# Four graph layers on one core: in two gather passes GpSimd waits behind each eight gathers until they have landed

## The reference

```python
def _gat(x, src, dst, W, a_src, a_dst, b, concat, n):
    H, C = a_src.shape
    h = (x @ W).reshape(n, H, C)
    s_src = (h * a_src).sum(-1)
    s_dst = (h * a_dst).sum(-1)
    e = jax.nn.leaky_relu(s_src[src] + s_dst[dst], NEG_SLOPE)
    m = jax.ops.segment_max(e, dst, num_segments=n)
    ex = jnp.exp(e - m[dst])
    denom = jax.ops.segment_sum(ex, dst, num_segments=n)
    alpha = ex / (denom[dst] + 1e-16)
    out = jax.ops.segment_sum(h[src] * alpha[:, :, None], dst, num_segments=n)
    ...
```

## Time and profile before

| what | us |
|---|---|
| time, median of 3 runs (lowest to highest) | 10376.22 (10362.24 to 10378.53) |
| span of the profiled execution | 10471.3 |
| first pass, first to last gather's start | 1414.9 to 2587.5 |
| second | 2831.3 to 4017.3 |
| third | 4278.4 to 5450.8 |
| fourth | 5701.3 to 7527.9 |

### The profile page before, as it was taken

One profiled execution on the slowest core, in us unless ns is written; L12 is line 12 of the kernel. 1 busy time (PEld: TensorE's weight loads), 2 busy tenths in 40 slices (PEclk: granted clock), 3 DMA queues, 4 the chain that ended last, 5 costly groups with the idle time before them and its releaser, 6 DMA issues. The chain is left out here.

```text
span 10471.3 us, 116347 instructions
## 1 busy us (share of the span) xinstructions
PE 6049.5 (58%) x41783; PEld 5358.8 (51%) x41783; DVE 3913.4 (37%) x8586; ACT 2215.5 (21%) x5791; POOL 5606.2 (54%) x5805
## 2 busy tenths in 40 slices
PE   3555634455456565455554666666669999943232
PEld 2445524444355554344442666665649999932222
DVE  5455523333334443344443333333332222232223
ACT  0000012222133332122220333333311111111111
POOL 6666366666666665666666566666540000036665
PEclk7555557766578876576665778888759999975555
DMA  4554252221133331233322444444319888821111
GB/s 160 168 169 166 81 43 54 55 53 48 41 94 98 99 97 38 78 102 94 103 77 66 120 119 124 121 122 121 92 35 359 339 334 334 334 97 24 23 23 23
DMA packets 437827, 1237.73 MB, mean 118 GB/s; under 512 B 161169, under 2 KB 226706, under 8 KB 394048
## 3 DMA queue, kind: packets, MB, share of 16 engines
q1 hardware_dynamic: 200226, 740.56, 20.1%
q0 software_dynamic: 237024, 489.72, 17.8%
HBM read 1099.82 MB, written 127.51 MB: 117 GB/s over the span
## 5 line engine op out<-in xcount | busy, mean ns | idle before, releaser
L1252 PE MATMUL ps<-pool 128*106 128x128 f32 (+2 forms) x19344 | 3021.3, 319 | 1685.2 <-issue 1171.0
L1252 PEld LDWEIGHTS ps<-pool 128*106 128x106 f32 (+2 forms) x19344 | 2773.5, 196 | 1889.3 <-issue 1406.2
L1210 ACT ACTIVATE ACC<-ps 72x256 f32 (+1 forms) x2418 | 1012.2, 419 | 2573.8 <-remote 1653.5
L469 POOL DMA_INDIRECT ACC<-t,ACC x416 | 393.4, 946 | 1649.6 <-DVE ps L1781 1448.4
L757 POOL DMA_INDIRECT cnt_d<-pool x806 | 835.3, 1036 | 534.3 <-issue 221.8
L1279 POOL DMA_INDIRECT pool<-d_h,srcT_s x806 | 772.8, 959 | 610.1 <-PE ps L1252 321.1
L488 PE MATMUL ps<-pool 128*65 128x128 f32 (+1 forms) x2392 | 556.8, 407 | 768.4 <-issue 577.3
L1279 POOL DMA_INDIRECT pool<-b_h,srcT_s x806 | 764.3, 948 | 423.0 <-issue 213.7
L1279 POOL DMA_INDIRECT pool<-a_h,srcT_s x806 | 779.0, 967 | 394.7 <-issue 230.4
L1279 POOL DMA_INDIRECT pool<-c_h,srcT_s x806 | 765.8, 950 | 407.9 <-issue 228.5
L1153 DVE TENSOR_TENSOR pool<-pool,ps 128x1024 f32<-128x1024 f32 (+1 forms) x807 | 927.6, 1210 | 0.0
(11 more groups left out here) (299 smaller groups left out, 6293.4 us busy)
## 6 DMA issues: line engine op xcount, KB each, us to landing
ACC<-cnt_d SPq DMA_DIRECT2D x186, 1600.0 KB, 8.8
pool<-cnt_d SPq DMA_DIRECT2D x94, 1600.0 KB, 8.7
cnt_d<-pool SPq DMA_DIRECT2D x28, 3200.0 KB
ACC<-key_d SPq DMA_DIRECT2D x31, 1664.0 KB
ACC<-key_d SPq DMA_DIRECT2D x25, 2048.0 KB
pool<-seg_d SPq DMA_DIRECT2D x100, 129.0 KB
cnt_d<-pool POOLq DMA_INDIRECT x806
pool<-a_h,srcT_s POOLq DMA_INDIRECT x806
```

Source lines behind the costliest of these rows:

```text
L469: g.indirect_dma_start(out=gb[b][:, k, :], out_offset=None, in_=table, in_offset=bass.IndirectOffsetOnAxis(ap=idx[:, c:c + 1], axis=0)).th ...
L1210: a.activation(win[:, 0:NPL, bass.ds(reg, 128)], pl[0].rearrange("p (i c) -> p i c", c=128), ACT.Copy).then_inc(*(tile_out if last else A) ...
L1252: mm = t.matmul(o, gbr[:, tile % RT, M * i:M * i + M], oh, start=True, stop=True)
```

## The change

Each of the three landing semaphores becomes two, one for each half of a group. VectorE waits for both before it takes the scores, in all four passes. In the first and third pass (`layer in (0, 2)`) GpSimd waits behind every eighth gather until that half's eight have landed. That is 100 waits a pass, since the last group, of six, has none. Arithmetic, buffers and all other orders stay.

```diff
@@ in gat @@
-        gat_g = [dsig(f"gat_rows{j}") for j in range(3)]
+        gat_g = [[dsig(f"gat_rows{j}{i}") for i in range(2)] for j in range(3)]
...
+            def half_in(gi, i):
+                return gat_g[gi % 3][i].sem, g0[gi % 3][i] + 16 * sum(min(8, GR[x][1] - 8 * i) for x in range(gi % 3, gi + 1, 3))
@@ def vector_edge_scores(gi) @@
-                v.wait_ge(gat_g[gi % 3].sem, g0[gi % 3] + 16 * sum(GR[x][1] for x in range(gi % 3, gi + 1, 3)))
+                for i in range(len(halves(gi))):
+                    v.wait_ge(*half_in(gi, i))
@@ def gpsimd_pass() @@
                         g.indirect_dma_start(
                             out=gbr[:, c % RT, 0:RW], out_offset=None, in_=ht,
-                            in_offset=bass.IndirectOffsetOnAxis(ap=srcT[:, c:c + 1], axis=0)).then_inc(*gat_g[gi % 3].one())
+                            in_offset=bass.IndirectOffsetOnAxis(ap=srcT[:, c:c + 1], axis=0)).then_inc(
+                                *gat_g[gi % 3][(c - c0) // 8].one())
+                        if layer in (0, 2) and (c - c0) % 8 == 7:
+                            g.wait_ge(*half_in(gi, (c - c0) // 8))
```

More of the change, by code:

```diff
@@ L962, in gat @@
                 x.sent for x in (scale_mm, scaled, turned, turn_out, slot_hot, slot_mm, slot_add))
-            g0 = [x.sent for x in gat_g]
+            g0 = [[x.sent for x in y] for y in gat_g]
             l0 = [x.sent for x in lists_g]
```

## The result

The changed kernel takes 10486.35 us (median, 10475.56 to 10493.13), the kernel before 10376.95 beside it: ratio 1.0113, 95% interval 1.01 to 1.0125. It is 1.1% slower, where 0.8% faster was forecast. The time lies within the stated range.

A forecast was written before the change was run, and what follows sets the result against it. It took GpSimd's gathers slowing TensorE, which then stalls GpSimd, to bound the first and third pass. First pass -26, third -41, tails -18 give -85 us: 10376 - 85 = 10291 us, range 10240 to 10500.

The forecast's parts named there:

- What bounds the kernel now: First and third pass: gathers in a row slow TensorE, which withholds the ring's place; GpSimd stops 3.23 to 3.30 us a group.
- the crawl: TensorE's slow stretch within a group of the first pass: sixteen records in 12.6 us, ending some 3 us after GpSimd falls silent.
- the crawl is not the profiler's: Denies a rival: timed runs have no crawl, so 200 waits are pure cost, +250 us, 10626; chance 0.05.
- the crawl outlives a short silence: Rival, both passes: TensorE may need 3 us of silence, not 1.6; 24.6 us a group, +120 us, 10496; chance 0.21.
- The price of a wait: GpSimd, first and third pass: each wait for a landing costs 1.25 us, 125 us a pass; 1.31 the upper bound by one row.
- 1006 + 16: First pass without waits: 805 gather steps of 1.25 us take 1006 us, plus 16 us for gathers longer than the median.
- -26: Forecast change of the first pass, first to last gather, in us: 1147 against 1172.6.
- That the price is the same everywhere: The third pass was charged the same 125 us for its waits as the first, giving 1131 us against 1172.4, -41.
- The stalls: GpSimd's 48 stalls on TensorE would go; a group costs 22.5 us on GpSimd, and TensorE's own 19.6 us fits below it.
- The tails: What follows the last gather of the first and third pass, 48 us, becomes 9 us shorter, twice: -18 us.
- The base: Timed runs lie 95 us below the profiled execution, so the whole kernel's forecast starts from 10376: 10376 - 85 = 10291.
- 1147 and 1131: Forecast times in us from first to last gather of the first and third pass, against 1172.6 and 1172.4.

The follow-up runs named there:

- fill8: Changed kernel with each GpSimd wait replaced by six iotas that rewrite a list with its own values, waiting for no landing: ratio 1.0022.
- keys_short_b: Changed kernel with the third pass's key rows cut from 2,048 KB to 64 KB from the third load on, beside a kernel before of 10365.51 us: ratio 1.0006.
- half_late: Changed kernel, but GpSimd waits behind each eight gathers for the eight before those, beside a kernel before of 8999.24 us: ratio 0.9999.
- only4: Changed kernel with the waits behind every eighth gather in the fourth pass only, none in the first and third: ratio 1.0066.
- after_b: The changed kernel itself, measured again beside a kernel before of 10365.51 us: ratio 1.0107.

## Why the prediction was wrong

**What bounds the kernel now:** right as far as the runs reach. Gathers in a row slow TensorE, a real stop frees it, and the crawl is not the profiler's; what passes between them stays open. The runs add that a stop of 1.8 us every 10 us is enough (`fill8`), one of 0.6 us isn't, and one every 20 us isn't. The rival "the crawl outlives a short silence" is wrong, though its number, 10496, came nearest. It is by luck that the time lies in the stated range: the range went up to 10500 for that rival alone, and its 120 us came from elsewhere.

**The price of a wait** failed, in the first pass. I took 1.25 us, with 1.31 as "upper bound by this row", from VectorE reading 1.61 us behind the gather's end less 0.30. But GpSimd isn't VectorE: it goes on 1.87 us behind the gather's end (median of the pass's 100), so a wait costs 1.57 (and 1.54 by 307 us for 200 where there was no crawl). With that the same sum fits: 1006 + 16 + 157 = 1179 against the 1178.8 measured. 0.32 us, 100 times, is 32 us, which turns -26 into +6.

**That the price is the same everywhere** failed, in the third pass, and this is the largest error. 1006 + 157 = 1163 is what `keys_short_b` measures (1163.8). The changed kernel takes 97 us more: 23 of its 24 long stops behind the key rows, of 5.8 to 6.7 us instead of 1.8 (the first stands in `keys_short_b` too). In the prediction the price came from the first pass alone. The last sentence named the danger ("if a landing takes longer behind a silence") but not the place, though the page of before lists the load. Before, the ring of 48 tiles hid a late landing; who waits for it behind each eighth gather has no such cover. The page of `half_late`, where there was no crawl, gives the load's duration (issue line: transfers, KB each, median us to landing):

```profile
ACC<-key_d SPq DMA_DIRECT2D x25, 2048.0 KB, 8.7
```

Issued at 4874.20, that would end at 4882.9. The changed kernel's own packet records are closer: the load's last data packet ends at 4881.59, the gather's last packet, a completion, at 4881.59 as well, and GpSimd goes on at 4882.19. It is so in all 23 long stops behind a load of an odd group: the two end within 0.2 us of each other (0.005 at the median), and GpSimd goes on 0.6 us behind. Most of the delay is in the gather's own data. Its last data packet ends 4.84 us behind the gather's end at the median, where 1.27 is usual; its last completion comes 0.6 us later still. The Trainium skill, in "DMA: Bandwidth & Descriptors", section "Queues, rings and completion order", has a rule that bears on the last part: a DMA's semaphore increment lands only after every earlier write of the same DMA engine, those of other queues too. The trace agrees: the last completion ends with the load's last data. That can account for some 0.6 us of each long stop; that the gather's data are late as well is shown by the packets alone.

**The stalls.** They went, as said. But 2 x 1.57 us of stops stand in the place of 3.0 us of stall, and TensorE's own pace of 19.6 us wasn't reached because GpSimd's is now 20.0 + 3.1.

**The tails:** 39.7 us instead of 48.0 behind the first pass's last gather (2576.2 to 2615.9), -8.3 where -9 was forecast. In the third, -4.6 (43.5 against 48.1) where -9 was forecast.

**The base.** I took 95 us off the whole and nothing off the passes, as if the profiled execution were longer elsewhere. `only4` shows 1160.7 us at the base time that the median had. Against that the forecast's own 1147 and 1131 would have been gains of 14 and 30 us, not 26 and 41.

**The misses together,** in us: the forecast -85, the price +64 (2 x 32), the key rows +97, the base +24 (2 x 12), the third pass's tail +5 give +105, against the 109 measured.

**The sum again,** from runs of like base times (`after_b` less `only4`): first pass +12.7 and its tail -8.3 (39.7 against 48.0 us), third +100.3 and its tail -3.7 (43.3 against 47.0), in all +101; the kernels differ by 107. The semaphore halves cost nothing, as forecast.

## What to carry to other kernels

A wait for a landing is priced by the engine that waits, and by all transfers that are under way at that moment: list the large loads of other queues by issue time before such a wait is put anywhere. A stop that has to break up an engine's slowness is only worth it if it is shorter than the stall that it replaces; here both were 3.1 us a group, and every weaker stop gave back what it saved. Where a stop is all that is wanted, it must not be tied to a landing (`fill8` 1.0022 against 1.0107).

## What the runs showed of the hardware

While GpSimd issues indirect DMAs without a pause, TensorE's fp32 products go on, in stretches, at one record in 0.85 to 2.05 us (mean of each stretch, first pass of the kernel before). In the kernel before 41 of the 48 stretches of the first pass end with a pause of 1.8 us or more in the issuing. Pauses of 1.8 us behind each eighth gather leave none in that pass, whether GpSimd idles in them (changed kernel) or computes (`fill8`). The Trainium skill, in "SBUF — State Buffer", section "Who interferes with whom", says that a DMA never contends with a compute engine; the kernel before, set against the changed one and `fill8`, speaks against it here. The page speaks of ports, and no run shows that the two meet at one.

A small gather that is issued while a 2,048 KB load of another queue is under way lands with that load: GpSimd, waiting for it, goes on 6.07 us behind the gather's end instead of 1.86 (medians of 23 and 76 stops, third pass).

In one of the six groups of runs the slowness didn't exist: the kernel before took 8999 us, a group 20.0 us, and TensorE did 48 records in 7.04 us beside unbroken gathers. The same change costs there 3.5% even with short key rows. The same chip number stands on record with 8999.24 and with 10372.24 us. A tuning against this slowness can't be judged from one group of runs.

```profile
1605.71 7.04 PEld L1256 LDWEIGHTS ps<-pool 128*72 128x72 f32 x48
```
